# Attention with a feed-forward part on one core: the chain of row maxima spread over two periods, with both weighing chunks ahead of the low passes

## What is computed

```
xn = layernorm(x)
Q = xn @ proj_q[h];  K = xn @ proj_k;  V = xn @ proj_v
weights = softmax(Q K^T)          # over the 1024 keys, no scaling
Y = sum_h (weights V) @ proj_o[h]^T
ffn = sum_e (xn @ w1[e]) @ w2[e]  # 8 experts, no non-linearity
out = x + Y + ffn
```

## Time and profile before

| | us |
|---|---|
| median of 3 runs | 1873.73 (1873.28 to 1875.96) |
| profiled execution, its time | 1877.59 |
| profiled execution, its span | 1875.8 |
| mean granted PE clock | 0.991 |

### The profile page before, as it was taken

How to read it: one execution, slowest core, us unless ns; L and a number is a source line. 1 busy time by engine, 2 the same in 40 slices (tenths; PEclk the granted TensorE clock), 3 DMA queues, 4 the chain that set the end, 5 groups by cost and what they waited for, 6 DMA issues and landing times.

```text
span 1875.8 us, 46345 instructions
## 1 busy us (share of the span) xinstructions
PE 1746.9 (93%) x18910; PEld 1184.9 (63%) x18910; DVE 1344.9 (72%) x2858; ACT 1321.8 (70%) x1396; POOL 1347.7 (72%) x957
## 2 busy tenths in 40 slices
PE   7699999999999999999999999999999999999997
PEld 6466666666666666666666666666666666666664
DVE  4477777777777777777777777777777777776774
ACT  3477777777777777777777777777777777777774
POOL 1477777777777777777777777777777777777775
PEclk9899999999999999999999999999999999999999
DMA  7000000000000000000000000000000000000000
GB/s 205 1 2 1 2 2 13 2 2 2 1 13 1 2 2 2 13 2 2 2 7 8 1 2 1 7 7 2 1 2 13 2 2 2 1 13 2 2 2 12
DMA packets 16048, 16.71 MB, mean 9 GB/s; under 512 B 384, under 2 KB 12032, under 8 KB 15840
## 3 DMA queue, kind: packets, MB, share of 16 engines
q1 hardware_dynamic: 13760, 12.72, 2.3%
q10 hardware_dynamic: 2080, 1.05, 0.2%
HBM read 9.57 MB, written 4.19 MB: 7 GB/s over the span
## 4 chain that ended last, share of the span: by engine, by line
PE 58%; POOL 20%; DVE 11%; issue 8%; ACT 2%; DMA 0%; POOLq 0%; DVEq 0%; ACTq 0%; SPq 0%
POOL pr_lo L235 16%; PE t_ps L350 8%; PE t_ps L348 8%; PE t_ps L349 8%; PE s_ps L428 7%; PE s_ps L414 7%; PE s_ps L429 7%; PE turn_ps L439 3%; POOL xacc L247 2%; PE misc L348 2%; PE misc L350 2%; PE misc L349 2%; DVE key_max L615 2%; ACT pr_hi L321 2%; PE turn_ps L443 2%
## 5 line engine op out<-in xcount | busy, mean ns | idle before, releaser
L235 POOL TENSOR_TENSOR pr_lo<-pr,pr_hi 128x1024 f16<-128x1024 f32 x512 | 1091.4, 2132 | 486.8 <-ACT pr_hi L321 479.7
L314 ACT ACTIVATE pr<-s_ps,boost,scale 128x1024 f32<-128x1024 f32 x410 | 493.9, 1205 | 373.4 <-PE s_ps L429 373.4
L615 DVE TENSOR_REDUCE key_max<-s_ps 128x128 f16<-128x1024 f32 x410 | 498.0, 1215 | 88.2 <-PE s_ps L414 87.1
L321 ACT ACTIVATE pr_hi<-pr 128x1024 f16<-128x1024 f32 x512 | 540.5, 1056 | 12.3
L428 PE MATMUL s_ps<-g_lo,xT 128*128 128x128 f16 x4096 | 514.7, 220 | 0.1
L429 PE MATMUL s_ps<-g_hi,xT 128*128 128x128 f16 x4096 | 514.6, 220 | 0.0
L428 PEld LDWEIGHTS s_ps<-g_lo,xT 128*128 128x128 f16 x4096 | 401.7, 98 | 1.2 <-DVE g_lo L629 0.2
L429 PEld LDWEIGHTS s_ps<-g_hi,xT 128*128 128x128 f16 x4096 | 402.0, 98 | 0.0
L348 PE MATMUL t_ps<-pr_hi,xn_hi 128*128 128x512 f16 x1024 | 388.9, 380 | 2.0 <-POOL pr_lo L235 2.0
L349 PE MATMUL t_ps<-pr_lo,xn_hi 128*128 128x512 f16 x1024 | 388.9, 380 | 0.0
L350 PE MATMUL t_ps<-pr_hi,xn_lo 128*128 128x512 f16 x1024 | 388.6, 380 | 0.0
(11 more groups left out here) (109 smaller groups left out, 1982.1 us busy)
## 6 DMA issues: line engine op xcount, KB each, us to landing
out_dram<-xacc SPq DMA_DIRECT2D x16, 256.0 KB, 2.3
w_sb<-in_L_ffn_w_dram SPq DMA_DIRECT2D x1, 2048.0 KB, 12.7
xacc<-in_L_attn_x_dram SPq DMA_DIRECT2D x1, 576.0 KB, 7.7
pr<-in_L_attn_proj_q_dram ACTq DMA_DIRECT2D x1, 512.0 KB, 4.8
...
```

The lines of the kernel that those rows point to most:

```text
L235: pool.tensor_tensor(pr_lo[:, u % RING, :], pr32[:, u % PR, :], pr_hi[:, u % RING, :], ALU.subtract)\
L314: act.activation(pr32[:, u % PR, :], bank(banks(u)[0], 2), ACT.Exp, bias=boost[:, 0:1], scale=scale[:, 0:1]).then_inc(exp_done, 1)
L321: act.activation(pr_hi[:, u % RING, :], pr32[:, u % PR, :], ACT.Copy).then_inc(p_hi_ready, 1)
L615: dve.tensor_reduce(key_max[:, u % 2, 0, :], bank(banks(u)[0], 2).rearrange("p (t q) -> p q t", q=P), AX_X, ALU.max).then_inc(keys_max, 1)
```

## The change

PE's loop has the same matmuls in another order. The high pass and the low passes are cut into halves of one bank each. `max_to_row` of unit n-1 stands between the halves of the high pass of period n, a period later than before. Both chunks come next, then the first half of the low passes of unit n-1, then `turn_keys_max(n)`, then the second half. Each chunk has now one tile of keys. On `misc`, `project` moves to n mod 4 = 2, and the halves of `head_out` to 3 and to 0 of the next block; the waits that guard the bank move with them. DVE places the bias of unit n-1 at the start of period n and has its side work in two new places: `between_maxima` (behind the maximum of keys) and `before_bias` (behind the maximum of queries). ACT has `t_high` ahead of the exponentials and `g_high` behind them, one period later. POOL has `p_low` at the end of its period. One more period is run. The diff, without the parts of the layer norm and of the start that only move along:

```diff
@@ -255,16 +255,14 @@
             head_adds = ffn_adds = 0
             for n in range(PERIODS + 2):
                 k, at = divmod(n, 4)
-                if 1 <= n <= UNITS:
-                    p_low(n - 1)
                 if n == 2:
                     spread_max(1)
                 if n == 7:
                     spread_max(2)
-                if at == 3 and 0 <= k - 2 < BLOCKS:
-                    add_head(k - 2, 0, ffn_adds)
+                if at == 0 and 0 <= k - 3 < BLOCKS:
+                    add_head(k - 3, 0, ffn_adds)
                     head_adds += 1
-                if at == 0 and 0 <= k - 3 < BLOCKS:
+                if at == 1 and 0 <= k - 3 < BLOCKS:
                     add_head(k - 3, 1, ffn_adds)
                     head_adds += 1
...
@@ -278,6 +276,8 @@
                     pool.wait_ge(ln_hi, tile + 1)
                     pool.tensor_tensor(xn_lo[:, tile % KEEP, 1:D], xn32[:, 0, 1:D], xn_hi[:, tile % KEEP, 1:D],
                                        ALU.subtract).then_inc(xn_ready, 1)
+                if 1 <= n <= UNITS:
+                    p_low(n - 1)
 
         @block.scalar
         def _(act):
@@ -329,12 +329,12 @@
             g_high(0)
             for n in range(PERIODS):
                 k, at = divmod(n, 4)
-                if at == 1 and k + 1 < BLOCKS:
-                    g_high(k + 1)
+                if at == 1 and 0 <= k - 2 < BLOCKS:
+                    t_high(k - 2)
                 if 1 <= n <= UNITS:
                     exponentials(n - 1)
-                if at == 1 and 0 <= k - 2 < BLOCKS:
-                    t_high(k - 2)
+                if at == 2 and k + 1 < BLOCKS:
+                    g_high(k + 1)
                 if 1 <= n <= UNITS:
                     p_high(n - 1)
...
-            def high_pass(u):
+            def high_pass(u, half):
+
                 k, j = divmod(u, 4)
-                if j == 0:
+                if j == 0 and half == 0:
                     pe.wait_ge(g_hi_ready, k + 1)
                     pe.wait_ge(xT_ready, batch_tile(k) + NT)
-                queries = g_hi[:, k % 2, j * P:(j + 1) * P]
-                for n, at in enumerate(banks(u)):
-
-                    if u - 3 + n >= 0:
-                        pe.wait_ge(exp_done, u - 3 + n + 1)
-                    keys = batch_tile(k) + (0 if at == min(banks(u)) else HT)
-                    for i in range(HT):
-
-                        last = pe.matmul(s_ps[:, at * BANK + i * P:at * BANK + (i + 1) * P], x_hi(keys + i), queries,
-                                         start=i == 0, stop=False, skip_group_check=True)
-                last.then_inc(high_done, 1)
-
-            def low_passes(u):
+
+                if u - 3 + half >= 0:
+                    pe.wait_ge(exp_done, u - 3 + half + 1)
+                at = banks(u)[half]
+                keys = batch_tile(k) + (0 if at == min(banks(u)) else HT)
+                for i in range(HT):
+
+                    last = pe.matmul(s_ps[:, at * BANK + i * P:at * BANK + (i + 1) * P], x_hi(keys + i),
+                                     g_hi[:, k % 2, j * P:(j + 1) * P], start=i == 0, stop=False, skip_group_check=True)
+                if half == 1:
+                    last.then_inc(high_done, 1)
+
+            def low_passes(u, half):
+
                 k, j = divmod(u, 4)
-                if j == 0:
-                    pe.wait_ge(g_lo_ready, k + 1)
-                pe.wait_ge(bias_ready, u + 1)
-                q_hi, q_lo = g_hi[:, k % 2, j * P:(j + 1) * P], g_lo[:, k % 2, j * P:(j + 1) * P]
-                for at in banks(u):
-                    keys = batch_tile(k) + (0 if at == min(banks(u)) else HT)
-                    for i in range(HT):
-                        dst = s_ps[:, at * BANK + i * P:at * BANK + (i + 1) * P]
-                        pe.matmul(dst, x_hi(keys + i), q_lo, start=False, stop=False, skip_group_check=True)
-                        last = pe.matmul(dst, x_lo(keys + i), q_hi, start=False, stop=True, skip_group_check=True)
-                last.then_inc(scores_ready, 1)
+                if half == 0:
+                    pe.wait_ge(bias_ready, u + 1)
+                    if j == 0:
+                        pe.wait_ge(g_lo_ready, k + 1)
+                at = banks(u)[half]
+                keys = batch_tile(k) + (0 if at == min(banks(u)) else HT)
+                for i in range(HT):
+                    dst = s_ps[:, at * BANK + i * P:at * BANK + (i + 1) * P]
+                    pe.matmul(dst, x_hi(keys + i), g_lo[:, k % 2, j * P:(j + 1) * P],
+                              start=False, stop=False, skip_group_check=True)
+                    last = pe.matmul(dst, x_lo(keys + i), g_hi[:, k % 2, j * P:(j + 1) * P],
+                                     start=False, stop=True, skip_group_check=True)
+                if half == 1:
+                    last.then_inc(scores_ready, 1)
 
             def turn_keys_max(u):
                 pe.wait_ge(keys_max, u + 1)
@@ -443,20 +448,25 @@
                 pe.matmul(turn_ps[:, 2 * P:3 * P], minus_max[:, u % 2, :], ident16[:, :], start=True, stop=True)\
                   .then_inc(rowed, 1)
 
-            def weigh(k, t):
-                if t == 0:
-                    pe.wait_ge(p_lo_ready, 4 * k + 4)
-                    if k == 0:
-                        pe.wait_ge(f_copied, 1)
-                    else:
...
+            def weigh(k, t, first, rest):
...
+                dst = t_ps[:, :].rearrange("p (j c) -> p j c", j=4)
+                if first:
+                    if t == 0:
+                        pe.wait_ge(p_lo_ready, 4 * k + 4)
+                        if k == 0:
+                            pe.wait_ge(f_copied, 1)
+                        else:
+                            pe.wait_ge(t_lo_ready, k)
+                    pe.matmul(dst, xn_hi[:, tile, :], p_hi, start=t == 0, stop=False)
+                if rest:
+                    pe.matmul(dst, xn_hi[:, tile, :], p_lo, start=False, stop=False)
+                    done = pe.matmul(dst, xn_lo[:, tile, :], p_hi, start=False, stop=t == NT - 1)
+                    if t == NT - 1:
+                        done.then_inc(pv_done, 1)
...
-            def chunk(s):
-
-                if 2 <= s < 2 + E:
+            def chunk(s, first=True, rest=True):
+
+                if 2 <= s < 2 + E and rest:
                     fold_ffn(s - 2)
-                k, i = divmod(s - 12, 8)
+                k, t = divmod(s - 12, NT)
                 if 0 <= k < BLOCKS:
-                    if i < 6:
-                        weigh(k, i)
-                    if i == 6:
-                        weigh(k, 6)
-                        weigh(k, 7)
+                    weigh(k, t, first, rest)
@@ -490,49 +496,57 @@
             def work_on_misc(n):
...
                 k, at = divmod(n, 4)
-                if at == 0 and k + 1 < BLOCKS:
-                    if k >= 3:
+                if at == 1:
+                    if 0 <= k - 3 < BLOCKS:
                         pe.wait_ge(y_scaled, 2 * (k - 3) + 2)
-                    else:
-                        pe.wait_ge(g_lo_ready, k + 1)
-                    project(k + 1)
-                if at == 1:
-                    if k + 1 < BLOCKS:
-                        pe.wait_ge(g_lo_ready, k + 2)
                     if (tile := ffn_tile(n)) is not None:
                         pe.wait_ge(weights_ready, 3)
                         three_pass(misc[:, 0:D], x_hi(tile), x_lo(tile), f_hi[:, :], f_lo[:, :]).then_inc(ffn_ps, 1)
...
-                if at == 2 and 0 <= k - 2 < BLOCKS:
+                if at == 2 and k + 1 < BLOCKS:
                     if (tile := ffn_tile(n - 1)) is not None:
                         pe.wait_ge(ffn_scaled, tile + 1)
                     if (tile := turn_tile(n - 1)) is not None:
                         pe.wait_ge(xT_ready, tile + 1)
+                    pe.wait_ge(g_lo_ready, k + 1)
+                    project(k + 1)
+                if at == 3 and 0 <= k - 2 < BLOCKS:
+                    if k + 1 < BLOCKS:
+                        pe.wait_ge(g_lo_ready, k + 2)
+                    elif (tile := ffn_tile(n - 2)) is not None:
+                        pe.wait_ge(ffn_scaled, tile + 1)
                     if k == 2:
                         pe.wait_ge(weights_ready, 2)
                     pe.wait_ge(t_lo_ready, k - 1)
                     head_out(k - 2, 0)
-                if at == 3 and 0 <= k - 2 < BLOCKS:
-                    pe.wait_ge(y_scaled, 2 * (k - 2) + 1)
-                    head_out(k - 2, 1)
+                if at == 0 and 0 <= k - 3 < BLOCKS:
+                    pe.wait_ge(y_scaled, 2 * (k - 3) + 1)
+                    head_out(k - 3, 1)
 
             pe.wait_ge(weights_ready, 1)
             pe.wait_ge(w1_evacuated, E)
             project(0)
             for n in range(PERIODS):
                 if n < UNITS:
-                    high_pass(n)
+                    high_pass(n, 0)
                 if 1 <= n <= UNITS:
```

(56 more changed lines are left out.)

33 lines of the change are left out of this document (15 added, 18 removed).

## The result

The changed kernel takes **2122.38 us** (median of 4 runs, 2121.75 to 2122.79); the kernel before took 1873.78 us on the same chip (4 runs, 1873.28 to 1875.96). The ratio is 1.132, with a 95% interval of 1.1305 to 1.1332: 13% slower. The profiled execution after took 2122.77 us, of which its span is 2121.0. The forecast was 2107 us, with a range of 2085 to 2165.

What follows compares the result with a forecast made beforehand. The prediction saw PE, busy 93%, bounding the kernel before, and a ring through the exponential bounding the changed one: 92 + 499 x 3.99 (1991) + 9.7 + 15.8 = 2108.5 us of span, 2107 us as a median, range 2085 to 2165.

Steps and rivals of the forecast that it cites:

- stops for the maxima: PE's waits for DVE's maxima at turn and row: 0.41 us a period, removed, at most 205 us.
- The ring: High pass's second half through chunks, low passes and exponential to the next second half: 3.93 us, mean 3.99 with parted units.
- The release: From the exponential's end on ACT to PE's waiting matmul: 0.06 us taken; may be 0.03 or lose another 0.10.
- the ring doesn't close: Rival: PE passes the waiting second half, or the ring is below 3.52 us; period 3.11, 1668 us; chance 0.04.
- The second stop in series: Rival: a cover fails in one period of four, adding 0.2 to 0.5 us there; 2132 to 2167 us; chance 0.08.
- the covers over the low part and g_low: Spare time before PE needs POOL's low part (1.0 us) and g_low (ends 2.4, PE comes at 2.5).
- The clock: Rival: PE idle 22% of each period lowers its clock; 3310 us if held throughout; chance 0.02.
- The start: Time until the second half of unit 12's high pass begins: 92 us, bounds 87 to 100.
- POOL now begins them ahead of a pr_lo, not behind it: In the start, POOL begins two spreads of a maximum over partitions earlier: worth 3 to 8 us.
- The second term: In the start, the periods with the w2 folds get longer by the ring; no separate size given.
- The end: From unit 511's second half: 9.7 us to the last low part's end, then 15.8 us to the span's end.
- the step from span to median: Span 2108.5 us becomes 2110.3 as a profiled execution, less 3.9 above the median of runs: 2106.5.

Runs made afterwards that it cites:

- e2: Changed kernel with each exponential split into two of 512 columns, the next high pass's second half waiting only for the first: 1926.30 us.
- e4: Changed kernel with two of three passes of head_out left out, so the heads use one matmul each in place of three: 2123.47 us.
- e5: Changed kernel with the pass of the low part of the probabilities left out of the weighing, two of six large matmuls fewer per period: 2003.83 us.
- e6: Changed kernel with p_low back at the start of POOL's period, ahead of the two spreads and the additions: 2171.04 us.
- e9: Kernel before with only the low passes moved behind both chunks and the turn: 2690.28 us, ratio 1.434.

## Why the prediction was right

**What bounds the kernel.** The 0.41 us of stops for the maxima are gone, as said: from 100 to 2094 us PE waits for neither the turn's maximum nor the row's. That alone would have been worth up to 205 us.

**The ring.** It was taken as 3.93 us for an ordinary unit and 3.99 on the mean, from rows of the kernel before alone. Measured were 3.94 and 3.9988; a parted unit has 4.18. Every term has its row above. The 0.009 us that were missing make 4.4 us over 499 periods. The release, which was bounded by 0.03 and 0.16, was at 0.06, as in the earlier trace rows: 1009.30 + 1.20 to 1010.56.

**The rivals.** That the ring doesn't close would have given 1668 us. e2 and e4 speak against it from two sides: to release the bank early gives 196 us with PE's work unchanged, and to take work from PE outside the ring gives nothing. The second stop in series is not in the changed kernel, but the runs show how near it is: e2 finds it on POOL at a period of 3.51, e5 on DVE at 3.69, e6 by one move in POOL's order. The prediction named the covers over the low part and g_low, and did not see that the turn's slack of 0.25 us (1.96 against 1.71) is a second ring.

The clock did not fall. The window of the steady part has 1.00:

```profile
98.00:2094.00 1996.00, 1645.34 (x18237) 1162.13 (x18237) 1316.44 (x2739) 1273.69 (x1348) 1307.84 (x923) 1.00 0.01 3
```

PE is busy for 82% of it, as forecast. The Trainium skill, page "TensorE: Matmul & The Clock Gate", section "A second HAM failure mode: psum-queue depth-cycling", describes a clock that swings between its levels when a kernel cycles PSUM banks with short stops between groups of matmuls. The trace of the changed kernel, which does this in every period, disagrees (1.00 over 1996 us); that of e9 agrees, with a mean of 0.94.

**The start was mis-sized.** The second half of unit 12's high pass was to begin at 92 us (87 to 100); it began at 98.76. This is the largest miss, 6.8 of the 15 us between forecast and result. The sum had two terms for it. The first is "POOL now begins them ahead of a pr_lo, not behind it, which is worth 3 to 8 us". PE's stops behind the two spreads did shrink: before they were 6.04 and 8.08 us, ended by L621, and now they are 2.67 and 4.33. That is 7.1 us won. But the low parts now wait behind the spread, and the weighing waits for them:

```profile
53.68 9.35 POOL L235 TENSOR_TENSOR pr_lo<-pr,pr_hi 128x1024 f16<-128x1024 f32 x4 [6.96 <-issue]
84.36 2.11 POOL L235 TENSOR_TENSOR pr_lo<-pr,pr_hi 128x1024 f16<-128x1024 f32 x1 [7.46 <-issue]
```

```profile
61.00 0.61 PE L464 MATMUL t_ps<-pr_hi,xn_hi 128*128 128x512 f16 x1 [3.07 <-POOL pr_lo L235]
...
89.18 0.61 PE L464 MATMUL t_ps<-pr_hi,xn_hi 128*128 128x512 f16 x1 [4.50 <-POOL pr_lo L235]
```

These are 3.07 + 4.50 = 7.6 us. What the order on POOL is worth on balance can be read from e6, which has the old order and all the rest of the change. Its stops behind the spreads are 7.41 and 7.71 us, and its weighing waits once:

```profile
95.71 0.39 PE L464 MATMUL t_ps<-pr_hi,xn_hi 128*128 128x512 f16 x1 [2.72 <-POOL pr_lo L235]
```

That is 17.8 us against 14.6 in the changed kernel, so the term is 3.3 us, the low end of what was forecast. I had asked where the stop goes, and not who is next behind the moved step on POOL.

The second term, that the first periods get longer by the ring, was named and given no number. From the first high pass to unit 12's point PE stands for an exponential eight times, 6.0 us in all, where the kernel before has no such stop; the short stops for the maxima are 2.8 us fewer. All stops together are 23.7 us for 20.0 before. The stretch itself is 68.8 us (29.96 to 98.76) for 63.9 before (31.49 to 95.34). The clock, which was not in the sum, may be the rest: it was 0.50 from 60 to 65 us, and 0.75 on the mean of 80 to 98.7 us, where the kernel before had 0.86.

**The end and the scale.** From unit 511's second half to the end of the span it is 26.86 us for a forecast of 25.5: the last low part ends at 9.94 (9.7), and the rest takes 16.9 (15.8). Before the last chunks PE now stands 3.18 us, where it stood 2.00, and the first of them runs slow; whether this is all of the 1.1 us was not followed up. The last piece is the step from span to median. The forecast took 2.1 us off the span, since the profiled execution of before was 3.9 above its median; after, the median is 1.4 above the span. So the misses are 6.8 + 4.4 + 1.4 + 3.5 = 16.1 us, for the 15.9 between 2106.5 and 2122.4.
